# Edits at the seams of a four-stage image kernel, and the attention's first transposes by 64-query halves

## What is computed

```python
x = x + _L0_conv_ref(_gn(x), w_qkv, rel_h, rel_w)
x = x + _L1_conv_ref(_gn(x), offset_w, offset_b, mask_w, mask_b, dcn_w)
x = x + _L2_conv_ref(_gn(x), w1, w2, lin1_w, lin1_b, lin2_w, lin2_b)
x = x + _L3_conv_ref(_gn(x), w_hidden, b_hidden, w_dw, b_dw, w_out, b_out)
```

```python
val = gather(y0i, x0i) * w00 + gather(y0i, x0i + 1) * w01 + gather(y0i + 1, x0i) * w10 + gather(y0i + 1, x0i + 1) * w11
out = jnp.einsum('bkhwc,bkhw,ock->bohw', val, mask, w_r)
```

## Time and profile before

| | |
|---|---|
| median of 3 runs | 1958.37 us |
| lowest, highest | 1957.63, 1969.23 us |
| the profiled execution | 1955.2 us |
| its span, first to last instruction | 1953.4 us |
| mean granted TensorE clock | 0.968 |

### The profile page before, as it was taken

How to read it: one execution, slowest core, us unless ns; L and a number is a source line. 1 busy time by engine, 2 the same in 40 slices (tenths; PEclk the granted TensorE clock), 3 DMA queues, 4 the chain that set the end, 5 groups by cost and what they waited for, 6 DMA issues and landing times. The chain is left out here.

```text
span 1953.4 us, 66215 instructions
## 1 busy us (share of the span) xinstructions
PE 1802.8 (92%) x25775; PEld 1208.2 (62%) x25775; DVE 1170.6 (60%) x2331; ACT 1065.0 (55%) x3473; POOL 912.7 (47%) x930
## 2 busy tenths in 40 slices
PE   5999999999999996788889998877999999999999
PEld 3666666666666664455545554566947677767766
DVE  5289999999999994256555565542454344334443
ACT  2499999999999993666656666110221122112221
POOL 0189999899999994544444453000001122212221
PEclk9999999999999998999999999987889999999999
DMA  4500111101110001456555565250013111221110
GB/s 164 162 27 27 31 31 30 29 26 31 31 30 29 27 27 45 133 152 158 153 145 151 149 169 143 62 108 12 12 45 63 42 48 39 52 57 47 39 40 17
DMA packets 165112, 136.03 MB, mean 70 GB/s; under 512 B 92142, under 2 KB 148436, under 8 KB 164871
## 3 DMA queue, kind: packets, MB, share of 16 engines
q1 hardware_dynamic: 159175, 127.58, 24.8%
q0 software_dynamic: 3840, 4.94, 0.9%
q10 hardware_dynamic: 1920, 1.03, 0.2%
HBM read 74.01 MB, written 40.71 MB: 59 GB/s over the span
## 5 line engine op out<-in xcount | busy, mean ns | idle before, releaser
L449 ACT ACTIVATE at_probs<-at_sc,at_nmx 128x196 f32<-128x196 f32 x1152 | 481.9, 447 | 4.4 <-DVE at_nmx L375 4.4
L357 POOL TENSOR_TENSOR at_probs<-at_probs,at_rs 128x784 f32<-128x784 f32 x288 | 430.5, 1495 | 69.4 <-DVE at_rs L380 69.4
L375 DVE TENSOR_REDUCE at_nmx<-at_sc 128x4 f32<-128x784 f32 x288 | 280.2, 973 | 76.5 <-PE at_sc L475 72.3
L2054 POOL TENSOR_TENSOR fc_spo<-fc_prod 64x256 f32<-64x256 f32 x144 | 104.3, 724 | 382.2 <-DVE fc_prod L2113 376.8
L475 PE MATMUL at_sc<-at_kw,at_qw 32*128 32x196 f32 x2304 | 267.6, 350 | 2.4 <-POOL at_qw L346 1.1
L449 ACT ACTIVATION_READ_ACCUMULATOR at_probs<-at_sc,at_nmx 128x1 f32 x1152 | 262.4, 228 | 0.0
L1153 PE MATMUL dn_cps<-dn_ring,dn_wconv 32*32 32x192 f32 (+2 forms) x3840 | 196.3, 343 | 23.4 <-issue 18.2
L1421 DVE COPY dn_sampled<-dn_sps 128x432 f32<-128x432 f32 x192 | 107.4, 600 | 183.6 <-PE dn_sps L1194 183.6
L2196 PEld LDWEIGHTS fc_qps<-fc_wk,fc_xs 99*128 99x128 f32 x1728 | 199.4, 192 | 18.0 <-issue 14.7
L475 PEld LDWEIGHTS at_sc<-at_kw,at_qw 32*128 32x128 f32 x2304 | 181.9, 184 | 45.8 <-ACT at_probs L449 29.2
L2196 PE MATMUL fc_qps<-fc_wk,fc_xs 99*128 99x128 f32 x1728 | 207.1, 276 | 2.5 <-DMA fc_xs<-fc_xp 2.5
(11 more groups left out here) (175 smaller groups left out, 2760.2 us busy)
## 6 DMA issues: line engine op xcount, KB each, us to landing
fc_xs<-fc_xp SPq DMA_DIRECT2D x140, 120.0 KB
at_vs<-attention_values SPq DMA_DIRECT2D x288, 49.0 KB
near_corners<-dn_split SPq DMA_DIRECT2D x24, 486.0 KB
dn_stack<-near_corners SPq DMA_DIRECT2D x24, 432.0 KB
dn_patch<-near_pixels SPq DMA_DIRECT2D x24, 384.0 KB
dn_patch<-near_pixels SPq DMA_DIRECT2D x48, 192.0 KB
dn_offs<-near_maps SPq DMA_DIRECT2D x24, 243.0 KB
attention_values<-ap_vrow SPq DMA_DIRECT2D x21, 256.0 KB, 2.4
```

The costliest lines, as they stand in the source:

```text
L357: nc.gpsimd.tensor_tensor(probs[s][p][:, :, :, :], probs[s][p][:, :, :, :], rs[s][:, 2 * p:2 * p + 2, :].unsqueeze(3).broadcast_to([P, 2, ...
L375: nc.vector.tensor_reduce(nmx[s][:, 2 * p:2 * p + 2, :], sc[p][:, :, 0:2 * NK].rearrange("p b (j k) -> p b j k", j=2), AX.X, ALU.max, nega ...
L449: nc.scalar.activation(probs[s][p][:, b, j, :], sc[p][:, b, NK * j:NK * j + NK], ACT.Exp, bias=nmx[s][:, 2 * p + b, j:j + 1], accum_out=su ...
```

## The change

- Attention: pair 0 is turned in 64-query halves too, so both pairs use one form; its waits stand on a sem_inc; the copies out write in strides for pair 0 as well. SyncE saves x_sb to x_save in twelve pieces of 384 KB, one for each row of windows, and the stage's end waits for them.
- Near stage: the 24 saves go, and the residual's wait on them. Four constants are loaded in the statistics block, whose end waits for none; TensorE waits for them before its first transpose. The other five are loaded after the border stores, and TensorE and VectorE wait for them later. The far test comes ahead of the last residual and its moments; its transpose stands between the last contractions.
- Far stage: the restore block goes; stage_norm loads x_sb inside the test of `far`, and TensorE runs six keep-warm products of 144 columns in that block, whatever `far` is.
- Fourier stage: four keep-warm products at the start and not ten; nine at the end of part 1 in place of ten at the start of part 2; the copy to z2 ahead of Gelu; the transposes of z2 ahead of the correction's products; VectorE's `corr` after the copies of those transposes.

```diff
@@ -27,13 +27,14 @@
...
-def keep_warm(nc, bank, tile, n):
-    for _ in range(n):
-        nc.tensor.matmul(bank[:, 0:512], tile[:, 0:P], tile[:, 0:512], start=True, stop=True)
-def stage_norm(nc, name, x_sb, xpad, pad, far=None, x_dram=None, loads=(), zeroed=None, blocks=()):
+def keep_warm(nc, bank, tile, times):
+    for _ in range(times):
+        n = min(512, tile.shape[1])
+        nc.tensor.matmul(bank[:, 0:n], tile[:, 0:P], tile[:, 0:n], start=True, stop=True)
+def stage_norm(nc, name, x_sb, xpad, pad, far=None, x_dram=None, loads=(), zeroed=None, blocks=(), restore=None, idle=None):
@@ -48,6 +49,9 @@
...
             const_in = ctx.enter_context(nc.semaphore(name + "_const_in"))
+        if restore is not None:
+            restored = ctx.enter_context(nc.semaphore(name + "_restored"))
+            spare = ctx.enter_context(nc.psum_tensor(name + "_spare", [P, 512], F))
@@ -67,6 +71,9 @@
...
             with when(sp, far):
+                if restore is not None:
+                    sp.dma_start(x_sb[:, :], restore).then_inc(restored, 16)
+                    sp.wait_ge(restored, 16)
@@ -83,6 +90,8 @@
...
             with when(dve, far):
+                if restore is not None:
+                    dve.wait_ge(restored, 16)
@@ -113,6 +122,11 @@
...
+        if idle is not None:
+            @block.tensor
+            def _(pe):
+                keep_warm(nc, spare, idle[:, :, :].rearrange("p k n -> p (k n)"), 6)
@@ -144,7 +158,7 @@
...
-def stage_attention(nc, x_dram, x_sb, rowstats, wqkvT, rel, halves, headmask, ident_d, q_dram, v_dram):
+def stage_attention(nc, x_dram, x_sb, rowstats, wqkvT, rel, halves, headmask, ident_d, q_dram, v_dram, x_save):
@@ -283,6 +297,7 @@
...
             pv_done, keys_ready, res_step, halves_begun = sem("pv_done"), sem("keys_ready"), sem("res_step"), sem("halves_begun")
+            saved = sem("saved")
@@ -327,13 +342,22 @@
...
+                def save(row):
+                    sp.wait_ge(res_step, HEADS * NROW // 2 * (row + 1))
+                    sp.dma_start(x_save[:, BLK * W * row:BLK * W * (row + 1)], x_sb[:, BLK * W * row:BLK * W * (row + 1)]).then_inc(saved, 16)
...
                         values(w + 2)
+                    if w >= NROW and w % NROW == 5:
+                        save(w // NROW - 1)
...
                         queries(w // NROW + 1, w % NROW // HALFROW)
+                save(NROW - 1)
+                sp.wait_ge(saved, 16 * NROW)
@@ -382,10 +406,7 @@
...
                     wait(dve, pv_done, w, 1, -1)
-                    if p == 0:
-                        part = pts[s][p][:, 0, :, :, :, :].rearrange("p c j h q -> p (c j h) q")
-                    else:
-                        part = pts[s][p][:, :, :, :, 0, :].rearrange("p b c j q -> p (b c j) q")
+                    part = pts[s][p][:, :, :, :, 0, :].rearrange("p b c j q -> p (b c j) q")
@@ -434,10 +455,7 @@
...
                     wait(act, pv_done, w, 1, -1)
-                    if p == 0:
-                        part = pts[s][p][:, 1, :, :, :, :].rearrange("p c j h q -> p (c j h) q")
-                    else:
-                        part = pts[s][p][:, :, :, :, 1, :].rearrange("p b c j q -> p (b c j) q")
+                    part = pts[s][p][:, :, :, :, 1, :].rearrange("p b c j q -> p (b c j) q")
@@ -482,15 +500,12 @@
...
                 def transposed(w, p, s):
-                    if p == 0:
-                        may_transpose(w, 0)
+                    may_transpose(w, p)
+                    pe.sem_inc(halves_begun, 1)
...
                             for j in range(2):
-                                if p == 0:
-                                    o = P * (2 * c + j)
-                                    mm = nc.tensor.transpose(pt[b][0:HK, o:o + P], probs[s][p][:, b, j, HK * c:HK * c + HK], ident[:, :])
-                                for h in range(2 * p):
+                                for h in range(2):
@@ -519,8 +534,6 @@
...
                     if there(w):
-                        may_transpose(w, 1)
-                        pe.sem_inc(halves_begun, 1)
@@ -559,18 +572,8 @@
...
-def stage_deform_far(nc, x_sb, convw, biasr, coord, base_ix, dcn, ident_d, xn_d, table, x_save, far):
-    with ExitStack() as ctx:
-        restored = ctx.enter_context(nc.semaphore("df_restored"))
-        block = ctx.enter_context(nc.Block())
-        @block.sync
-        def _(sp):
-            with when(sp, far):
-                sp.dma_start(x_sb[:, :], x_save).then_inc(restored, 16)
-                sp.wait_ge(restored, 16)
+def stage_deform_far(nc, x_sb, rowstats, convw, biasr, coord, base_ix, dcn, ident_d, xn_d, table, x_save, far):
@@ -583,7 +586,7 @@
...
             xp = ctx.enter_context(nc.sbuf_tensor("df_xp", [P, TY, TX], F))
-            stage_norm(nc, "gnf", x_sb, xp, EDGE, far)
+            stage_norm(nc, "gnf", x_sb, xp, EDGE, far, restore=x_save, idle=rowstats)
@@ -951,13 +954,12 @@
...
-def stage_stats(nc, name, rowstats, agg, loads, zeros):
+def stage_stats(nc, name, rowstats, agg, loads, const_in, zeros):
...
         step_done = ctx.enter_context(nc.semaphore(name + "_step_done"))
-        const_in = ctx.enter_context(nc.semaphore(name + "_const_in"))
@@ -965,7 +967,6 @@
...
                 sp.dma_start(to, source).then_inc(const_in, 16)
-            sp.wait_ge(const_in, 16 * len(loads))
@@ -994,7 +995,7 @@
...
-def stage_deform_near(nc, x_sb, rowstats, convw, convb, sel, bars, dcn, shifts, caps, ident_d, pixels, map_d, corner_d, x_save, far):
+def stage_deform_near(nc, x_sb, rowstats, convw, convb, sel, bars, dcn, shifts, caps, ident_d, pixels, map_d, corner_d, far):
@@ -1011,10 +1012,11 @@
...
         border = sb("border", [P, EDGE * REACH * PBLK])
-        stage_stats(nc, "gn1", rowstats, agg, zeros=(ring[:, :, :], border[:, :]),
-                    loads=((wconv[:, :, :], convw), (bconv[:, :], convb), (selw[:, :], sel), (shift[:, :], shifts), (cap[:, :], caps),
-                           (wd[:, :, :], dcn), (ident[:, :], ident_d),
-                           *((stack[i][DATA:STACK, :, :, :, :].rearrange("p b t k n -> p (b t k n)"), bars) for i in range(2))))
+        first_in, weights_in = sem("first_in"), sem("weights_in")
+        stage_stats(nc, "gn1", rowstats, agg, zeros=(ring[:, :, :], border[:, :]), const_in=first_in,
+                    loads=((ident[:, :], ident_d), (wconv[:, :, :], convw), (bconv[:, :], convb), (shift[:, :], shifts)))
+        late = ((selw[:, :], sel), (cap[:, :], caps), (wd[:, :, :], dcn),
+                *((stack[i][DATA:STACK, :, :, :, :].rearrange("p b t k n -> p (b t k n)"), bars) for i in range(2)))
@@ -1034,7 +1036,7 @@
...
         cps = psum("cps", [P, 512])
-        chunk_ready, saved = sem("chunk_ready"), sem("saved")
+        chunk_ready = sem("chunk_ready")
@@ -1099,13 +1101,10 @@
...
-            def save(t):
-                if t >= 1:
-                    sp.wait_ge(saved, 16 * t)
-                sp.dma_start(x_save[:, t * DPX:(t + 1) * DPX], x_sb[:, t * DPX:(t + 1) * DPX]).then_inc(saved, 16)
...
                 sp.dma_start(pixels[y:y + EDGE, :, :, :].rearrange("r q k n -> (r q k n)").rearrange("(p n) -> p n", p=P), border[:, :]).then_inc(border_out, 16)
+            for to, source in late:
+                sp.dma_start(to, source).then_inc(weights_in, 16)
@@ -1119,7 +1118,6 @@
...
             for t in range(DTILES):
-                save(t)
@@ -1212,6 +1210,7 @@
...
+            pe.wait_ge(first_in, 64)
@@ -1226,6 +1225,7 @@
...
                 conv(4, u)
+            pe.wait_ge(weights_in, 80)
@@ -1242,9 +1242,9 @@
...
                         sample(s)
-            pe.wait_ge(least_ready, DTILES + 2)
-            nc.tensor.transpose(cps[0:1, 0:P], lowest[:, 1:2], ident[:, :]).then_inc(conv_done, 1)
+                    elif k == 2:
+                        pe.wait_ge(least_ready, DTILES + 2)
+                        nc.tensor.transpose(cps[0:1, 0:P], lowest[:, 1:2], ident[:, :]).then_inc(conv_done, 1)
@@ -1423,7 +1423,6 @@
...
                 dve.wait_ge(contracted, t + 1)
-                dve.wait_ge(saved, 16 * (t + 1))
@@ -1465,8 +1464,7 @@
...
             moments(DTILES - 2)
-            residual(DTILES - 1)
-            moments(DTILES - 1)
+            dve.wait_ge(weights_in, 80)
@@ -1475,6 +1473,8 @@
...
             nc.vector.tensor_scalar(far, bottom[:, :], 1.0, None, ALU.is_ge)
+            residual(DTILES - 1)
+            moments(DTILES - 1)
@@ -1671,7 +1671,7 @@
...
             def _(pe):
-                keep_warm(nc, yps[0], x_sb, 10)
+                keep_warm(nc, yps[0], x_sb, 4)
@@ -1722,6 +1722,7 @@
...
                 mm.then_inc(z_done, 1)
+                keep_warm(nc, yps[1], x_sb, 9)
@@ -1773,10 +1774,10 @@
...
                     gather_modes(act, b)
+                act.wait_ge(moved, 16 * B)
+                nc.scalar.copy(z2[:, :, :, :], z[:, :, :, :].rearrange("p k y r -> p y r k")).then_inc(sorted_, 1)
...
```

(15 more changed lines are left out.)

8 lines of the change are left out of this document (4 added, 4 removed).

## The result

The changed kernel takes 2309.55 us (median of 4, 2299.85 to 2313.82), the kernel before 1961.05 (median of 4). The ratio is 1.176, 95% interval 1.171 to 1.182: 348.5 us slower. Forecast were 1931 us, 27 less than the 1958 shown then. Both the size and the sign were wrong.

The account below looks back on a forecast made before the run. Attention was taken as bound by a two-window chain through GpSimd, the seams by single engines' waits. Terms summed to −26.9: 1955.2 to 1928.3, plus 3.2 gave 1931 us; 8-in-10 range 1908 to 1946.

Parts of the forecast that it names:

- the term for attention's transposes: Attention: halving the first pair's transposes saves TensorE 0.44 us per window, mostly becoming idle time; −1 us, bounds 0 and −28.
- A slow clock: Rival at the Fourier start: after the shorter warm-up the clock might stay half through the width transforms; up to +50, chance 0.03.
- the middle term: Fourier middle: nine warm products move into the idle after part 1; −7.6 us, or +2 if the clock falls again.
- Waits of their own, and the saves: Attention: moving the first pair's waits to their own instruction and adding twelve x_sb saves costs 0 us.
- Seam to the near stage: Attention to near: statistics block closes without waiting for all loads, so first transpose comes earlier; −4.6 us, bounds −5.3 and 0.
- Near stage: Near stage: dropping 24 stores cuts DMA traffic by 7% and shortens TensorE's waits; −5 us, bounds 0 and −15.
- End of near: Near's end: far test moves ahead of last residual and moments, −0.9 us; one skipped far-stage block goes, −1.3 us.
- Fourier start and middle: Fourier stage: four warm products instead of ten at the start, −4.8 us; nine moved into part 1's idle, −7.6 us.
- as early as the staging: Fourier middle's larger bound: the first mix comes as early as the staging allows; −8.4 us.
- Fourier's end part: Fourier tail: z2's copy goes ahead of Gelu and its transposes ahead of the correction's products; −1.7 us, bounds −2.05 and 0.
- PSUM copies as the limit: Attention: a skill rule that copies out of PSUM may limit, so none of 63 us comes beyond what ScalarE has free.
- The seams give little: Rival at the seams and later stages: each gained wait passes to the next; terms sum to −12, 1946 us, chance 0.18.

Follow-up runs that it names:

- e9_wide_start_timed: Changed kernel with the first pair's transposes in 128-query form in the first 8 of 144 windows only; median 1915.4 us, ratio to before 0.985.
- e6_halves_pause: Changed kernel, first eight windows with 128-query first-pair transposes, plus 150 sem_inc on TensorE ahead of window 68; 2127.65 us in one execution.
- e1_wide_first: Changed kernel with the first pair's transposes and their copies back in 128-query form, all else as changed; median 1930.57 us, ratio to before 0.988.
- e2_halves_alone: Kernel before with only the first pair's 64-query halves and their waits on a sem_inc, no saves or seam edits; 2331.45 us in one execution.
- e10_twice_pause: Changed kernel with each half transpose of the first pair made twice, plus 150 sem_inc ahead of window 68; 1956.41 us in one execution.
- e11_all_wide_pause: Changed kernel with both pairs' transposes in 128-query form, plus a TensorE pause in the middle of attention; 1994.49 us in one execution.
- e12_wide_pause_timed: Changed kernel with all first-pair transposes in 128-query form, plus 150 sem_inc ahead of window 68, timed; median of 10 1959.47 us, ratio 0.998.
- e7_wide_pause: Changed kernel with all first-pair transposes in 128-query form, plus 150 sem_inc ahead of window 68, first run; 1972.05 us in one execution.
- e13_longer_warm_timed: Changed kernel, halves everywhere, with two more keep-warm products ahead of each of windows 1 to 3; median 1923.16 us, ratio 0.988.

## Why the prediction was wrong

**The failed step is the term for attention's transposes**, −1 us with bounds 0 and −28. That a shorter stream would become idle time was right: with the clock high, e9_wide_start_timed has 4.50 us a window, TensorE idle by what was saved, and GpSimd's spread as the wait. Wrong was that work taken off TensorE costs nothing. Without the longer transposes this loop did not win back its clock once it had fallen (e6_halves_pause), and at the loop's start it did fall. The earlier trace rows show the loop at 1.00, and the working went on as if that were a property of the loop; with halves it is one of two states in which the loop can stay. The price, 2.78 us a window by 139 windows, was nowhere among the bounds. What a half clock costs could be read before, as the keep-warm products' 0.86 us against 0.43: twice the TensorE stream of a window, 2 × (4.50 − 0.44) = 8.1 us, is an estimate of 3.6 us more a window, 520 in all, where 387 were measured.

**A slow clock was among the rivals, at the wrong place.** It stood at the Fourier stage, with at most +50 us and a chance of 0.03. At the stage's start the argument held: eight records carried TensorE over the rise (transposes 4.7 us behind the stage's start). In the middle it held in part: through the idle of 2.3 us ahead of the mix the clock stayed at 1.00, but it fell at about 1720.8, inside the mix, and was back at about 1724.2, where before it was 1.00 from 1366 to 1390. That is the case for which the middle term had named +2; by an estimate from these times it cost at most 1.7 us (3.4 us at half clock). The same doubt belonged first of all to attention, where the edit takes most work off TensorE, in 144 windows.

**Waits of their own, and the saves**: nothing, as forecast (e1_wide_first: 4.50 us a window; a save of 384 KB lands 2.7 us after issue).

**Seam to the near stage**: −5.2 for −4.6. The last save's landing delayed the block by the 1.4 us expected (1141.01 is 2.81 behind the last residual, 1.37 before), VectorE then waits 0.33 us and not 7.02, and TensorE's first transpose waits for the last of the four constants, as the row at 1144.36 has it.

**Near stage**: −11.2 in this pair of profiles for −5, but this can't be called confirmed. From the first transpose to the last contraction kernels with these edits take 494.6 us (the changed one), 509.6 (e1_wide_first) and 481.1 (e9_wide_start_timed), against 505.9 before; and e2_halves_alone, which has none of the near stage's edits, takes 496.8. So a single profile moves by more than the term with nothing edited. The clock in the stage differs too (0.95 and 0.99 above). What the saves' traffic was worth stays open. The Trainium skill's Runtime: NRT & Kernel Launch, "Instruction fetch mechanics", by which the term would have been 1, is neither shown nor refuted.

**End of near, Fourier start and middle**: −2.3, −5.3 and −8.4 for −2.2, −4.8 and −7.6. These sums from rows held to within 1 us each. The middle reached its bound "as early as the staging", −8.4: the first mix waits for ScalarE's copy (fb_wst), not for the warm products.

**Fourier's end part**: the two edits gave −2.4 for −1.7 (hidden-layer products' last weight load to the first back transform, 5.9 us and 3.6). The further 7 us to the Fourier convolution were not forecast: the clock averages 0.91 there and not 0.83. In e1_wide_first, with the same code, it is 0.82 and the whole stretch is 2.9 us shorter than before, not 9.8, so the edits are not shown to be the cause of the 7.

**PSUM copies as the limit**: the Trainium skill's TensorEngine Tiling (Array Packing), "PSUM Bottleneck", pointed the right way as to gain, none at full clock, though the wait that ends last is GpSimd's spread and not a copy. It says nothing of a loss.

**The prediction's own sums** come out but for two in the rivals. The slow clock's is 1978 as written, 1955 − 27 + 50, and 1981 only with the 3.2 us added. "The seams give little" takes −5 for the middle and −0.5 for the tail, whose stated bounds are −6.3, or +2 with a fall of the clock, and 0. Neither bears on the miss.

## What to carry to other kernels

Before work is taken off TensorE in a long loop, ask what its granted clock does at the loop's start and what would mend a fall. A loop that is seen at 1.00 may only have entered so, and time saved on an engine that isn't the limit can cost the clock of it. Leave the transposes as they are where shorter ones win nothing, as here at full clock; where they do win, put the longer form, or a few products nobody reads, into the first windows. Test the loop with a deliberate pause: whether it comes back is a property that an undisturbed run at the high clock doesn't show. And bound a term by what the clock's other level would make of the stage, even where every row shows the high one.

## What the runs showed of the hardware

A loop that keeps TensorE in work without a pause in the records for 530 us at half clock need not get its full clock back (e6_halves_pause, 530.00 of 530.00 at 0.50), though the same instructions hold the full clock for 600 us with TensorE idle 9% of the time (e9_wide_start_timed, 455.55 of 500). From the end of the pause, winning back took 11 us with the first pair's halves made twice (e10_twice_pause), 33 with both pairs wide (e11_all_wide_pause), 59 and 67 with one (e12_wide_pause_timed, e7_wide_pause), and did not happen with halves alone. These are one profile each; only the kernel with one wide pair was run more than once with the pause. The Trainium skill's TensorE: Matmul & The Clock Gate, Part 4, "PE-mode transpose", states that transposes don't count as busy for the clock in the way that products do. These runs don't bear it out: e10_twice_pause and e6_halves_pause differ behind the pause only in repeated transposes, and one has its clock back in 11 us, the other not in the 530 us to the end of attention.

What stays open: whether the length of one uninterrupted run of transposes or the amount of work in a window of attention decides. All kernels that won the clock back in the loop have more of both. Open too is why the clock falls at the loop's start. In before it fell under the last warm products and was back at about 100.1; in the changed kernel it fell behind them; in e1_wide_first, e9_wide_start_timed and e13_longer_warm_timed it did not fall there. The changed kernel has one profile, and the mean clocks of its four executions, 0.751 to 0.755, say that all of them lost it about as early.
